# A four-layer graph network on one core: the first eleven steps and the last pairs of its software pipeline written out in orders of their own

## The reference, cut to what matters

```
h = relu(layernorm(x)); x = x + L0(h)    # 8 heads: q, k, v = h @ w_qkv; softmax(q k^T, masked by adj) v;
                                         # o = that @ w_proj + b_proj;  L0 = o + (layernorm(o) * gamma + beta)
h = relu(layernorm(x)); x = x + L1(h)    # rel = adj^T * (q k^T); rel / row norm of rel; times v
h = relu(layernorm(x)); x = x + L2(h)    # h W; e = leaky_relu(s1 + s2) * adj; softmax(e) h W + beta h W; elu
h = relu(layernorm(x)); x = x + L3(h)    # (adj h) W + bias
```

## Time and profile before

| | us |
|---|---|
| median of 3 runs | 1447.32 |
| the profiled execution, its own time | 1446.77 |
| span of the profiled execution, first to last instruction | 1445.0 |
| from the start to the first masked minimum (L759) of pair 0 | 23.09 |
| from there to the one of pair 11, the filling and the first full steps | 209.08 |
| from pair 11 to pair 59, 48 full steps | 1042.57 |
| from pair 59 to pair 63 | 86.63 |
| from pair 63 to the end | 83.63 |

### The profile page before, as it was taken

The page is one execution under the profiler, slowest core; times in us unless marked ns, Lnnn a source line. Parts: engine busy times, 40 slices in busy tenths (PEclk is TensorE's granted clock), DMA queues, the critical chain, the costliest instruction groups (busy, mean ns, idle before and its releaser), DMA issues.

```text
span 1445.0 us, 45699 instructions
## 1 busy us (share of the span) xinstructions
PE 1385.2 (96%) x14092; PEld 1300.0 (90%) x14092; DVE 1368.0 (95%) x6094; ACT 1233.1 (85%) x3911; POOL 1014.0 (70%) x1684
## 2 busy tenths in 40 slices
PE   4999999999999999999999999999999999999986
PEld 4888999999999999999999999999999999999975
DVE  3899999999999999999999999999999999999986
ACT  5889988988988888889888889889888889889854
POOL 5577767777777777777777777777777777777663
PEclk9999999999999999999999999999999999999999
DMA  3000100101100101100001000000001001001001
GB/s 113 17 17 17 31 17 31 31 17 31 31 17 31 31 17 31 31 17 31 30 18 31 26 22 31 26 22 31 24 24 31 22 25 31 21 27 31 13 20 37
DMA packets 38112, 39.76 MB, mean 28 GB/s; under 512 B 2416, under 2 KB 37488, under 8 KB 37872
## 3 DMA queue, kind: packets, MB, share of 16 engines
q1 hardware_dynamic: 37872, 36.84, 8.1%
HBM read 20.05 MB, written 16.78 MB: 25 GB/s over the span
## 4 chain that ended last, share of the span: by engine, by line
DVE 47%; PE 32%; issue 16%; POOL 2%; ACT 1%; DMA 0%; DVEq 0%; POOLq 0%; SPq 0%; ACTq 0%
PE bank L330 12%; DVE stats L749 9%; DVE s_prod L802 8%; PE mid L330 7%; PE mid L374 4%; PE bank L386 4%; DVE x L881 4%; DVE masked L759 3%; DVE x_exp L871 3%; DVE x L897 3%; DVE o L900 3%; DVE m_t_lo L817 2%; PE bank L540 2%; DVE o_gam L793 2%; DVE mean_var L753 2%
## 5 line engine op out<-in xcount | busy, mean ns | idle before, releaser
L583 ACT ACTIVATE probs<-masked,neg_max 128x128 f32<-128x128 f32 x1024 | 397.7, 395 | 30.0 <-DVE neg_max L759 30.0
L759 DVE CUSTOM_DVE_ANT_0 masked<-mid,mask 128x128 f32<-128x128 f32 x1024 | 226.9, 287 | 11.4 <-issue 11.4
L802 DVE CUSTOM_DVE_ANT_0 s_prod<-h,wa_rows 128x256 f32<-128x256 f32 x256 | 198.2, 826 | 2.9 <-issue 2.9
L583 ACT ACTIVATION_READ_ACCUMULATOR probs<-masked,neg_max 128x1 f32 x1024 | 198.2, 194 | 0.0
L749 DVE BATCH_NORM_STATS2 stats<-x 128x6 f32<-128x256 f32 x384 | 143.1, 413 | 0.2
L365 PE MATMUL bank<-ident,probs 128*128 128x128 f32 x1024 | 139.7, 274 | 2.5 <-POOL probs L984 1.2
L975 POOL TENSOR_TENSOR xb<-x,b_proj_beta 128x512 f32<-128x512 f32 x64 | 82.5, 1290 | 81.4 <-DVE o_res L875 81.4
L955 POOL TENSOR_TENSOR var_eps<-mean_var,eps 128x2 f32<-128x2 f32 x192 | 43.0, 224 | 137.0 <-DVE mean_var L753 137.0
L958 POOL TENSOR_TENSOR rstd<-var_eps,minus_half 128x2 f32<-128x2 f32 x192 | 133.3, 694 | 0.0
L365 PEld LDWEIGHTS bank<-ident,probs 128*128 128x128 f32 x1024 | 114.2, 140 | 10.9 <-POOL probs L984 1.6
L970 POOL TENSOR_TENSOR h_t_lo<-h_t_full,h_t_hi 128x512 fp32r<-128x512 f32 x64 | 81.8, 1278 | 45.1 <-ACT h_t_hi L645 45.1
(11 more groups left out here) (157 smaller groups left out, 5983.6 us busy)
## 6 DMA issues: line engine op xcount, KB each, us to landing
x<-in_x SPq DMA_DIRECT2D x64, 256.0 KB, 2.8
out_x<-x SPq DMA_DIRECT2D x64, 256.0 KB, 2.2
w_qkv_sb<-in_w_qkv SPq DMA_DIRECT2D x1, 768.0 KB, 5.2
w_v_sb<-in_w_v_t SPq DMA_DIRECT2D x1, 256.0 KB, 5.4
w_proj_sb<-in_w_proj SPq DMA_DIRECT2D x1, 256.0 KB, 5.8
w_q_sb<-in_w_q SPq DMA_DIRECT2D x1, 256.0 KB, 6.4
w_k_sb<-in_w_k SPq DMA_DIRECT2D x1, 256.0 KB, 7.0
w_gat_x<-in_w_gat SPq DMA_DIRECT2D x1, 256.0 KB, 5.8
```

The costliest lines, as they stand in the source:

```text
L583: last = act.activation(probs[:, r, s], masked[:, r, s], ACT.Exp, scale=-1.0, bias=neg_max[:, r, s:s + 1], accum_out=sums[:, r, s:s + 1])
L759: last = dve.tensor_tensor_reduce(out=masked[:, r, s], in0=mid[:, r, s * N:(s + 1) * N], in1=mask[:], scale=1.0, scalar=LARGE, op0=ALU.add ...
L802: last = dve.tensor_tensor_reduce(out=s12_prod[:, b, j], in0=h2[:, i5, b], in1=wa_rows[:, j], scale=1.0, scalar=0.0, op0=ALU.mult, op1=ALU ...
```

## The change

The body of `step` is cut into one function per operation and engine, named after what it makes and called with the number of the pair: `z0T_of(p)`, `k_of(p)`, `S_of(p)`, `v_of(p)` on PE, `ex0_of(p)` to `ex3_of(p)` on ACT (the exponentials), `mt0_of(p)` to `mt3_of(p)` on DVE (the masked minima), `s12_of(p)`, `pn0_of(p)` to `pn3_of(p)` on POOL, and so on. `run` and `streams` are gone. Each engine now calls `first_steps()`, then `step(t)` for t = 11 to 58, then `last_steps()`. `step(t)` calls the functions in the order of the old list. `first_steps` and `last_steps` are lists of calls, each engine with its own, in which the operations of one step stand in another order than in the next and may stand among those of a neighbouring step; the same operations are in them as before, each once, and the functions for the constants stand among them. SP's stream is unchanged.

```diff
-            run(pe, step, [(0, first_weights), (0, value_weights), (1, fold), (3, folded_weights),
-                          (1, next_weights), (5, last_weights), (2, wa_rows_made)])
+            def first_steps():
+                first_weights(); z0T_of(0); k_of(0); q_of(0); S_of(0); z0T_of(1); value_weights(); v_of(0)
+                fold(); k_of(1); next_weights(); pT0_of(0); pT1_of(0); q_of(1); pT2_of(0); pT3_of(0); S_of(1)
+                AV_of(0); proj_of(0); z0T_of(2); v_of(1); k_of(2); pT0_of(1); pT1_of(1); wa_rows_made()
...
+            first_steps()
+            for t in range(11, PAIRS - 5):
+                step(t)
+            last_steps()
...
             def first_steps():  # vector
+                st0_of(0); first_constants(); st0_of(1); h0lo_of(0); next_constants(); mt0_of(0); mt1_of(0)
+                mt2_of(0); mt3_of(0); h0lo_of(1); ei0_of(0); last_constants(); st0_of(2); ei1_of(0); mt0_of(1)
...
             def first_steps():  # gpsimd
+                rs0_of(0); rs0_of(1); next_constants(); xb_of(0); pn0_of(0); pn1_of(0); pn2_of(0); pn3_of(0)
+                rs0_of(2); last_constants(); xb_of(1); pn0_of(1); pn1_of(1); rsO_of(0); pn2_of(1); pn3_of(1)
```

```diff
+            def x1_of(p):
+                i = p % 2
+                dve.wait_ge(o_gam_ready, done(p))
+                dve.wait_ge(o_res_ready, done(p))
+                dve.wait_ge(ln_rstd[LN_O], done(p))
+                if p > 1:
+                    dve.wait_ge(x2_ready, done(p - 2, 2))
...
+            def x3_of(p):
+                i = p % 2
+                dve.wait_ge(x2_exp_ready, done(p))
+                wait_two_before(dve, x3b_ready, p)
+                wait_two_before(dve, h3_ready, p)
```

More of the change, by code:

```diff
@@ new lines, in attT_of, with v1_of @@
+            def attT_of(p):
+                pe.wait_ge(att_norm_ready, done(p, 2))
+                bank_free(pe, (h_hi_ready[1], p + 2, 1), (max_ready[1], p + 4, 1), (e_leaky_ready, p, 2),
+                          (att_t_ready, p - 1, 1))
+                for b in range(2):
+                    last = pe.transpose(att_bank[:, b * N:(b + 1) * N], att_norm[:, b], ident[:])
+                last.then_inc(att_t_psum, 1)
+            def v1_of(p):
+                pe.wait_ge(h_lo_ready[1], done(p))
+                bank_free(pe, (max_ready[2], p + 2, 1), (v1_ready, p - 1, 1))
+                rows(halves(v1_bank), h_t[1], w_v_p, 0, D).then_inc(v1_psum, 1)
@@ new lines, in ssq_of, with v_of @@
+            def ssq_of(p):
+                pe.wait_ge(rel_sq_ready, done(p))
+                for b in range(2):
+                    last = pe.matmul(rel_bank[:, 256 + b:257 + b], rel_sq[:, b], ones[:, 0:1], start=True, stop=True)
+                last.then_inc(sum_sq_psum, 1)
+            def v_of(p):
+                pe.wait_ge(h_lo_ready[0], done(p))
+                bank_free(pe, (max_ready[0], p, 1), (q_ready, p, 1), (v0_ready, p - 1, 1))
+                rows(halves(v_bank), h_t[0], w_qkv_p, 2 * D, D).then_inc(v0_psum, 1)
@@ new lines, in ex3_of, with h2_of @@
+            def ex3_of(p):
+                act.wait_ge(max_ready[3], done(p))
+                wait_before(act, probs_t_psum[3], p)
+                exps(3).then_inc(probs_ready[3], 1)
+            def h2_of(p):
+                i = p % 2
+                act.wait_ge(shift_ready[2], done(p))
+                wait_two_before(act, m_psum, p)
+                for b in range(2):
+                    last = act.activation(h2[:, i, b], x2[:, i, b], ACT.Relu, bias=shift[2][:, b:b + 1], scale=rstd[:, 2, b:b + 1])
+                last.then_inc(h2_ready, 1)
```

1130 lines of the change are left out of this document (696 added, 434 removed).

## The result

The changed kernel takes 1449.62 us (median of 22 runs, 1447.18 to 1451.44), the kernel before 1447.12 us on the same chips (22 runs). The ratio is 1.0015, 95% interval 1.0008 to 1.0021. So it is slower by 2.5 us in the medians and 2.2 us by the ratio, inside the 0.2% that I had called no change, and 10 us above the forecast of 1439.6 us, outside its range. The profiled execution has a span of 1448.2 us against 1445.0.

The account below looks back on a forecast made before the run. PE and DVE, both nearly full, hand work to each other, so reordering can only remove idle time. Terms summed to -7.7 us from 1446.77 us, 1439.1, adjusted to the median as 1439.6 us; range 1433.5 to 1446.0.

Parts of the forecast that it names:

- step of pair 1: Pair 0's work after its mark: h_t_hi ahead of ACT's exponentials and DVE's late constants give back 1.1 us.
- The start: Before pair 0's mark: moments made ahead of the constants let z start earlier on ACT, 3.6 us less.
- The hole on ACT: Sign of being right: some 2 us idle on ACT before the first exponential, as h_t_hi waits for v.
- The emptying: Behind pair 63's mark: fewer slow s_prod products and filled DVE idle time, 3.5 us less.
- Both of its parts: Emptying: 2.1 us from sparing two slow s_prod products, 1.4 us from moments filling DVE's idle time before s_prod.
- the price of the two waits: DVE, each step: the added waits are satisfied long before and cost only their issue, 0.2 us more in all.
- Rival 4: DVE, each step: the added waits are exposed and cost 3.2 us instead of 0.2, giving 1442.6 us; chance 0.06.
- Ten full steps, 1.2 us less: Pairs 6 to 10 and 59 to 63: new orders use PE's 0.21 us slack per step, 1.2 us less.
- Pair 1's v: PE makes v behind the projection instead of ahead; v's 1.66 us is half exposed, 0.8 us more.
- k of pair 3: PE makes k ahead of v1 and g, sparing ACT's wait for k, 0.9 us less.
- upper bound of 7 us for the emptying: Most the emptying could gain: DVE's idle 18.0 us less the 11.6 left idle by the last pair's chain.
- rival 3: Every planned step: h_t_hi behind v and ahead of exponentials on ACT blocks; 0.8 us a step gives 1453 us; chance 0.06.

Follow-up runs that it names:

- e5: Kernel before's step orders; only the start changed: DVE makes pair 0's moments before the first constants, POOL the first two roots before all constants: 1444.80 us.
- e1: The kernel before with only the two added DVE waits, ahead of x1 and x_up: 1451.04 us, ratio 1.0024.
- e8: Kernel before's order for all steps up to pair 63, then the remaining work in the new lists' order: 1446.37 us, ratio 0.9988.
- e15: The kernel before with only the added wait ahead of x_up: 1447.08 us, ratio 0.9993.
- e12: e11 plus 21 unread transposes on PE's idle spots in the emptying; three pairs of PE waits also changed order: 1442.27 us, ratio 0.9962.
- e14: The changed kernel plus the 21 unread transposes of e12, with its changed order of PE waits: 1448.94 us, ratio 1.0007.
- e16: e13 plus the 21 unread transposes of e12, with its changed order of PE waits: 1442.77 us, ratio 0.9962.
- e11: Kernel before's order with the start of e5 and the last orders of e7, no extra waits in the middle: 1441.89 us, ratio 0.9967.
- e13: Changed kernel, no middle waits, pair 1's h_t_hi and v in old places, old order for pairs 6 to 58, last orders of e7: 1441.68 us.
- e3: The changed kernel without the added waits in the middle and with the last steps in the old order: 1448.09 us, ratio 1.0005.
- e4: The changed kernel without the added waits in the middle and with the first eleven steps in the old order: 1448.57 us, ratio 1.0009.
- e7: e4 with DVE making m_t_lo of pair 56 ahead of x1 and the moments of pair 59: 1446.32 us, ratio 0.9990.
- e18: Kernel before's order in every step, with the start of e5 and the emptying of e8: 1440.53 us, ratio 0.9958.
- e17: e13 with the steps of pairs 59 to 63 in the old order and the emptying of e8: 1441.50 us, ratio 0.9965.

## Why the prediction was wrong, step by step

The lead in the profiles, split at the marks, beside the terms of the forecast (us, positive is a loss):

| term | forecast | profile after | what the runs showed |
|---|---|---|---|
| start, to pair 0 | -3.6 | -4.5 | -3.5: the mark lies at 22.2 on average in six profiles with the old start, at 18.7 in fourteen with the new; in the time of e5 2.3 to 2.7 are left |
| step of pair 1 | +1.1 | +1.8 | h_t_hi costs 1.5 |
| step of pair 2 | +0.8 | +1.6 | v costs 2.0 |
| pairs 3 to 5 | -1.5 | -0.9 | step of pair 3: -0.3 with the moved start alone (15.86 to 15.56), -0.3 by the new order (15.29); step of pair 5: -0.3 |
| pairs 6 to 11 | -0.6 | +1.8 | waits 0.3, orders 0 to 1 |
| middle, waits | +0.2 | +3.0 | +3.0 in e1, which has nothing but the waits; the one at x_up 0 |
| pair 56 to the end | -4.1 | +0.4 | emptying about -3, five steps ahead of it about +2, two falls more about +1.8 |
| sum | -7.7 | +3.2 | |

**Right.** The start, by its mechanism and, over many profiles, by its size; the old kernel's profile happened to have a late start of 23.09. The hole on ACT and its cause. The emptying: -3.5 forecast, -3.2 to -3.5 shown where the clock is alike and the steps ahead are old. Both of its parts are there in e8, from the mark of pair 62 to the end (101.2 us against 105.1): DVE is busy 2.3 us less with the same instructions, where I had 2.1, and idle 1.6 us less, where I had 1.4. But the first is a difference. The s_prod products take 4.2 us less there; z, att_norm and x1 take 2.3 us more together. In the changed kernel, behind pair 63's mark, the slow s_prod products are 2 (0.79 and 1.25 us) instead of the 4 of the earlier trace rows, 2.5 us less of DVE, and att_norm and x1 take 1.4 us more; in the step of pair 61, x1 took 1.62 us instead of 0.85, beside POOL's x3b (1316.96 to 1318.23). A product that is moved out of POOL's way leaves its place to another. The rule for which the prediction named the Trainium skill, "SBUF — State Buffer", "Who interferes with whom" (a DVE instruction with two SBUF inputs is held off by a GpSimd instruction that reads SBUF, for that instruction's whole length), has x1 in its reach too, whose o_gam and o_res lie in SBUF; the trace agrees, with the 1.62 us of x1.

**The step that failed first: the price of the two waits.** The prediction took "the low end, since the row shows two waits hidden". The row was x_up's, and for x_up it holds (e15). I carried it over to x1, for which PE's scores wait, through m_t_lo, in every full step. I had 0.2 us for the two; e1 is slower by 3.5 us by its ratio, 3.0 of them between pairs 11 and 56. Rival 4 had the size about right, 3.2 us, and I gave it 0.06. A cost of 0.05 us in a loop of 62 turns on the path is worth more than a microsecond of idle time in the filling, and it was the one part of the change that stood in every step.

**Ten full steps, 1.2 us less.** I took the unused 0.21 us of a step as what a list could win, and wrote that a blocked step costs 0.2 to 0.8 us. One of them, m_t_lo behind x1, stands ahead of the scores for 1.83 us. "DVE makes m_t_lo ahead of x1" is true of most places in the new lists, but not of m_t_lo of pairs 53, 56 and 58; the runs moved that of pair 56 alone. I had read the rule and not each place.

**Pair 1's v.** I priced it at half of v's 1.66 us because the projection waited anyway. It costs 2.0: h_t_hi of pair 2 waits for v on ACT, and k, q and the exponentials stand behind it. The wait passes through two engines, and in full.

**The clock.** The prediction had no term for it. In the profile the emptying stood at 0.98, which was one fall, and I passed over it. The two more in the changed kernel's profile are some 1.8 us of the miss there. Over all executions it is less, 1.3 falls and 1.1 us by the mean granted clocks (0.9961 against 0.9976). Why the changed kernel has more of them is not shown.

**The other terms.** The 0.9 us for k of pair 3 was too much; the runs leave 0.3 for the whole new order of that step. And the upper bound of 7 us for the emptying is 6.4 by its own terms (18.0 less 11.6); nothing else hung on it.

**The rivals.** None of them came out. The size of rival 4 did, and the lead was eaten by places that rival 3 looked for in the wrong spot (h_t_hi in every step). The forecast range held no case in which several small losses meet.

## What to carry to other kernels

Price a change in the loop's body first, however small, and multiply it by the turns; 0.05 us a turn on the path cost 3.5 us (e1), more than the 2.3 to 2.7 us that the moved start won (e5). A hand-made order for the filling or emptying should be taken in parts: here the moved start and the reordered emptying gave 6 us, and three misplaced calls among more than a thousand, with one added wait, took all of it and more. Before the idle time of a stretch is compared between two profiles, compare the clock in it, and compare the mean clock of all executions. And look at the stretches in which an experiment should change nothing: they showed that the fillers had come with another change.

## What the runs showed of the hardware that I had not expected

- A further satisfied wait costs 0.05 us ahead of one DVE instruction (x1) and nothing ahead of another (x_up), measured by e1 and e15 in some 60 steps each.
- The order of waits has a price too: with three pairs of waits on PE in the other order a full step takes 0.02 to 0.03 us more (e12, e14 and e16 against e11, the changed kernel and e13). Which of the three costs it was not tested.
- TensorE's granted clock fell from full to half, 2.4 to 1.2 GHz, behind idle spots of PE of 1.0 to 2.5 us among dense work (before: 1.02 and 2.48 us idle ahead of the fall at 1379.9; after: 1.38 us ahead of the one at 1401.7), for some 3.4 or 6.8 us, and not each time: in e3, idle spots of 1.02 and 1.41 us ahead of 1377.8 were followed by none. In the emptying a fall costs 0.9 to 1.0 us. In the step of pair 1 it costs about 1.6 right behind its first mark (15.0 us in e4 and e5 against 13.4 to 13.5 in before, e1, e7 and e18), 1.1 at 28.5 us (14.6 in e8), and nothing at 27.5 in e3, where that step takes 15.2 us as in the changed kernel without a fall.
- A DVE product with one input tensor in SBUF was slow at times too: z took 1.38 us instead of 0.41 once in the emptying of e8, e17 and e18, in e8 beside POOL's x3b (1362.92 to 1364.35).
- Full steps of one profile are alike to 0.02 us or so, except that every sixteenth takes 22.00 us; with the waits at x1 (e1 and the changed kernel) these are 22.05, 22.33 and 22.11. In the kernels of the changed form without the waits in the middle, two more steps are long (22.0 and 21.9 us, those of pairs 22 and 24), 0.5 us in all; the changed kernel and e14 don't have them. The cause was not sought.
